# A channel-attention, causal-attention and two-layer network kernel: six images of a group as one schedule, and the first image's second normalisation moved into the attention

## The reference

```
x = x + proj(channel_attention(x))          # 8 heads; l2-normed q and k; 24 x 24 softmax per head
t = tokens(x)                               # 1024 x 192
t = t + causal_attention(layer_norm(t))     # 6 heads of 32, 1024 x 1024 scores, scale 1/sqrt(192)
z = layer_norm(t)
h = quant(z @ sign(W1).T + b1)              # 768 wide; 5 groups of W1's rows have their own mean
t = t + quant(gelu(h) @ sign(W2).T + b2)
x = image(t)
# quant: five groups of 6 images share one maximum (gamma): clip(a * 128 / (gamma + 1e-5), -128, 128);
#        images 30 and 31 belong to no group and get 0 from both quants
```

## Time and profile before

| | |
|---|---|
| Median of 3 runs | 4847.52 us (4846.21 to 4848.08) |
| Profiled execution | 4839.8 us, span 4838.0 us |
| Mean granted TensorE clock | 0.963 |
| Busy: PE, PE weight loads, DVE, ACT, POOL | 4119.7, 2991.4, 3333.5, 2714.9, 363.5 us |
| DMA | 161.62 MB, mean 33 GB/s |

### The profile page before, as it was taken

The page is one execution under the profiler, slowest core; times in us unless marked ns, Lnnn a source line. Parts: engine busy times, 40 slices in busy tenths (PEclk is TensorE's granted clock), DMA queues, the critical chain, the costliest instruction groups (busy, mean ns, idle before and its releaser), DMA issues.

```text
span 4838.0 us, 114787 instructions
## 1 busy us (share of the span) xinstructions
PE 4119.7 (85%) x39153; PEld 2991.4 (62%) x39208; DVE 3333.5 (69%) x6327; ACT 2714.9 (56%) x5911; POOL 363.5 (8%) x374
## 2 busy tenths in 40 slices
PE   3889887888898878989897979898888989887978
PEld 2666665566666636766674566666646666664565
DVE  3667676677676757767676777676667767676776
ACT  1555555555555555555556555565555555556655
POOL 0000002000000020000002000000020000002000
PEclk8999999999999989999999999999999999999999
DMA  1211111011111201111111011122101111111011
GB/s 49 52 35 34 35 34 34 0 47 35 35 34 40 55 0 40 34 35 34 35 36 32 0 47 34 35 49 46 34 0 40 34 35 34 35 41 27 0 40 41
DMA packets 48698, 161.62 MB, mean 33 GB/s; under 512 B 12420, under 2 KB 12934, under 8 KB 48006
## 3 DMA queue, kind: packets, MB, share of 16 engines
q1 hardware_dynamic: 48134, 154.39, 13.3%
HBM read 28.52 MB, written 25.17 MB: 11 GB/s over the span
## 4 chain that ended last, share of the span: by engine, by line
PE 61%; DVE 15%; issue 15%; ACT 4%; POOL 2%; DVEq 1%; DMA 1%; ACTq 0%; SPq 0%; POOLq 0%
PE PT L667 10%; PE OUT L687 9%; PE S L653 5%; PE PT L776 5%; PE S L703 4%; DVE nmax L1137 4%; DVE work L370 4%; PE S L613 3%; PE FR L613 3%; PE S L745 2%; PE FR L561 2%; PE S L561 2%; DVE XT L1032 1%; PE FR L620 1%; PE S L620 1%
## 5 line engine op out<-in xcount | busy, mean ns | idle before, releaser
L886 ACT ACTIVATE work<-S,nmax 128x256 f32<-128x256 f32 (+7 forms) x1536 | 1139.0, 742 | 1119.1 <-DVE nmax L1137 1056.7
L1137 DVE TENSOR_REDUCE nmax<-S 128x1 f32<-128x256 f32 (+7 forms) x1536 | 1156.4, 753 | 844.8 <-PE S L655 829.0
L667 PE MATMUL PT<-ident,work 128*128 128x128 f32 x6912 | 1110.2, 281 | 220.1 <-DVE work L370 188.7
L667 PEld LDWEIGHTS PT<-ident,work 128*128 128x128 f32 x6912 | 748.4, 142 | 434.6 <-DVE work L370 262.6
L370 DVE COPY work<-PT 128x512 f32<-128x512 f32 (+3 forms) x1536 | 892.0, 582 | 57.6 <-PE PT L667 52.7
L653 PE MATMUL S<-KS,QS 128*128 128x512 f16 (+3 forms) x1152 | 330.3, 342 | 106.8 <-issue 57.8
L890 ACT ACTIVATE work<-PT 128x512 f32<-128x512 f32 (+3 forms) x768 | 331.4, 432 | 53.5 <-PE PT L667 53.4
L655 PE MATMUL S<-causal,identb 128*128 128x128 bf16 x1536 | 341.7, 222 | 0.0
L653 PE MATMUL S<-odd 128*128 128x512 f16 (+3 forms) x1152 | 315.4, 328 | 16.7 <-ACT work L886 14.7
L1172 DVE TENSOR_REDUCE gm<-S 128x1024 f32 (+1 forms) x180 | 220.0, 1222 | 154.6 <-PE S L745 154.4
L745 PE MATMUL S<-odd,W1b 128*128 (+1 forms) x1080 | 297.4, 385 | 12.1 <-ACT odd L920 9.5
(11 more groups left out here) (198 smaller groups left out, 6037.7 us busy)
## 6 DMA issues: line engine op xcount, KB each, us to landing
X<-in_x SPq DMA_DIRECT2D x32, 768.0 KB, 5.3
odd<-hi_z SPq DMA_DIRECT2D x128, 192.0 KB, 4.2
odd<-odd SPq DMA_DIRECT2D x128, 192.0 KB, 4.2
out_y<-work SPq DMA_DIRECT2D x64, 384.0 KB, 3.9
QS<-hi_z SPq DMA_DIRECT2D x64, 192.0 KB, 3.6
QS<-odd SPq DMA_DIRECT2D x64, 192.0 KB, 4.0
KS<-hi_z SPq DMA_DIRECT2D x64, 192.0 KB, 4.7
KS<-odd SPq DMA_DIRECT2D x64, 192.0 KB, 4.7
```

The source lines that it names most:

```text
L667: last = tr(bank[:, P * (j - c0):P * (j - c0) + P], PS[m % 2][:, m // 2 % 2, P * j:P * j + P], ident[:, :])
L886: A(PS[n % 2][:, n // 2 % 2, 0:w], S[:, n % 2, 0:w], ACT.Exp, bias=nmax[:, n % MAXES:n % MAXES + 1], accum_out=rowsum[:, sum_col(n):sum_co ...
L1137: v.tensor_reduce(nmax[:, n % MAXES:n % MAXES + 1], S[:, n % 2, 0:P * (qtile(n) + 1)], AX.X, ALU.max, negate=True).then_inc(max_made, 1)
```

## The change

1. The slots are written out for all six images of a group (`GROUP` = 6, 288 units, 296 slots) and no inner loop runs over pairs; `groups` calls the body once a group. Images 30 and 31 keep the two-image form: `attention(LAST, 2, 1)`. All semaphore counts go by group and image (`after(g, u, per, n)`).
2. `EARLY` lays parts of the tail into the last slots of the six-image form. On DVE: the first image's statistics in slots 270 and 271 and their aggregate in 272, the second image's in 283, 284 and 285. On ACT: the first image's normalisation and rounding in 277 and 278. On PE and ACT: its four turns and copies in 286 to 289. Scores end with slot 287. The turns use the two banks of the front (`FB`) and the rounded parts a new place `zcat0` in `odd`, in KS1's first heads, which are read for the last time in slot 263. On POOL the first image's part is written out ahead of the loop over the other five.
3. In the tail, PE no longer waits for the last `add_to_t1`, but for the last exponential and oT copy, makes no turns before the loop over y1, and goes to y1 at once. ACT waits for the stacking DMAs and then normalises images 1 to 5. DVE makes no statistics ahead of the first maximum.

```diff
+EARLY = {270: "stats0", 271: "stats1", 272: "aggregate", 277: "norm0", 278: "norm1", 283: "next_stats0",
+         284: "next_stats1", 285: "next_aggregate", 286: "turn0", 287: "turn1", 288: "turn2", 289: "turn3"}
...
+zcat0 = odd[:, 6144:9216].rearrange("p (a b) -> p a b", a=TT)
...
             with e.Fori(0, NGROUPS) as g:
-                with e.Fori(0, GS // 2) as p:
-                    body(e.snap(g * (GS // 2) + p), p)
+                body(g)
                 tail(g)
...
 # POOL, tail
+                ln2(g * GS, zcat0)
+                with pool.Fori(1, GS) as b:
+                    ln2(pool.snap(g * GS + b), zcat)
...
 # PE, at the end of a slot
+                    if images == GS and EARLY.get(n, "").startswith("turn"):
+                        k = int(EARLY[n][-1])
+                        if k < 2:
+                            wait_freed(pe, g, GS, STEPS[k - 2])
+                            pe.wait_ge(z2lo_made, after(g, 0, 2, 3))
+                        else:
+                            pe.wait_ge(z2lo_made, after(g, 0, 2, 4))
+                            pe.wait_ge(z2t_made, after(g, 0, 4, k - 1))
+                        turn_z(FB[k % 2], k, zcat0).then_inc(z2t_full, 1)
...
 # PE, tail
-                pe.wait_ge(t1_step, nb * (GS // 2 * 3 * NB2))
+                pe.wait_ge(exp_made, nb * (GS * UNITS))
+                pe.wait_ge(oT_made, nb * (GS * NBI))
...
-                for k in range(4):
-                    turn_z2(g * GS, k)
...
 # ACT, at the end of a slot
+                    if images == GS and EARLY.get(n, "").startswith("norm"):
+                        act.wait_ge(rstd2_made, after(g, 0, 4, 4))
+                        norm_z2(0, g * GS, int(EARLY[n][-1]), zcat0)
+                    if images == GS and EARLY.get(n, "").startswith("turn"):
+                        k = int(EARLY[n][-1])
+                        put_z2(0, g * GS, k, FB[k % 2])
...
 # ACT, tail
-                with act.Fori(0, GS) as b:
+                for st in stacked:
+                    act.wait_ge(st, (g + 1) * (GS * STACKS) + STACKS)
+                    alone(act)
+                with act.Fori(1, GS) as b:
...
 # DVE, at the end of a slot
+                    if images == GS and n in EARLY:
+                        part = EARLY[n].removeprefix("next_")
+                        b = int(part != EARLY[n])
+                        if part == "stats0" and b:
+                            dve.wait_ge(ln2_step, after(g, 0, 16, 16))
+                            alone(dve)
+                        if part.startswith("stats"):
+                            stats2(b, range(4 * int(part[-1]), 4 * int(part[-1]) + 4))
+                        elif part == "aggregate":
+                            aggregate2(g * GS + b)
...
 # DVE, tail
-                for b in range(2):
-                    if b:
-                        dve.wait_ge(ln2_step, g * (GS * 16) + 16)
-                    stats2(b, range(TT))
-                    aggregate2(g * GS + b)
```

More of the change, by code:

```diff
@@ L74, in unit_of, with last_slot, triples_at, batches_at @@
     return 6 * (k // 2) + k % 2 + 2 * hh
[L77 to L84, removed]
+def last_slot(images):
+    return 12 * (NBI * images - 1) + BACK_AT
+def triples_at(images, slot):
+    return [k for k in range(KI * images) if 6 * (k // 2) + PV_AT[k % 2] == slot]
+def batches_at(images, slot, at):
+    return [j for j in range(NBI * images) if 12 * j + at == slot]
 def batch_tiles(j):
@@ L332, in groups, with after, wait_freed @@
             with e.Fori(0, NGROUPS) as g:
-                with e.Fori(0, GS // 2) as p:
-                    body(e.snap(g * (GS // 2) + p), p)
+                body(g)
                 tail(g)
[L337 to L343, removed]
+        LAST = NGROUPS
+        def after(g, u, per, n):
+            return g * (GS * per) + (u * per + n)
+        def wait_freed(e, g, u, step, less=0):
             b = bank_of(step)
-            e.wait_ge(front_free[b], after(pair, u, FRONT_FREES[b], freed(step) - less))
-        def of_pair(pair, per, n):
-            return pair * per + n
+            e.wait_ge(front_free[b], after(g, u, FRONT_FREES[b], freed(step) - less))
         def fronts_at(slot, run, parts, fronts):
@@ L420, in _, with body @@
             front(0, 0, True)
-            def pair_body(pair, p):
-                for u in range(2):
-                    front(pair, u + 1, True)
+            def body(g):
+                for u in range(GS):
+                    front(g, u + 1, True)
             def group_tail(g):
@@ L493, in _, with body, ln2 @@
             front(0, 0)
-            def pair_body(pair, p):
-                for u in range(2):
-                    front(pair, u + 1)
+            def body(g):
+                for u in range(GS):
+                    front(g, u + 1)
             def group_tail(g):
-                with pool.Fori(0, GS) as b:
-                    ab = pool.snap(g * GS + b)
+                def ln2(ab, zc):
                     pool.wait_ge(ln2_step, ab * 16 + 16)
@@ L521, in group_tail @@
                 pool.partition_all_reduce(gam2, run2, P, RMAX).then_inc(gam2_made, 1)
-            groups(pool, pair_body, group_tail)
+            groups(pool, body, group_tail)
             front(LAST, 1)
@@ L549, in front_part @@
                     if k == 0:
-                        pe.wait_ge(x_in, after(pair, u, 16, 16))
+                        pe.wait_ge(x_in, after(g, u, 16, 16))
                     for t in range(2):
@@ L585, in front_part @@
                 elif name == "u":
-                    pe.wait_ge(xsoft, after(pair, u, XSOFT, XSOFT))
+                    pe.wait_ge(xsoft, after(g, u, XSOFT, XSOFT))
                     for j in range(2):
@@ L605, in front_part @@
                     if k % 2 == 0:
[L606 removed]
+                        pe.wait_ge(zlo_made, after(g, u, 2, k // 2 + 1))
                     last = turn_z(FR, k)
@@ L825, in front_part @@
                 if name == "xexp":
-                    act.wait_ge(xsoft, after(pair, u, XSOFT, 6))
+                    act.wait_ge(xsoft, after(g, u, XSOFT, 6))
                     for j in range(2):
```

297 lines of the change are left out of this document (148 added, 149 removed).

## The result

| | before | after |
|---|---|---|
| Median | 4846.86 us (4846.07 to 4848.08, 4 runs) | 4679.76 us (4676.95 to 4687.25, 4 runs) |
| Profiled execution | 4839.8 us, span 4838.0 | 4680.1 us, span 4678.3 |
| Mean granted TensorE clock | 0.963 | 0.977 |

The ratio is 0.9657, interval 0.9641 to 0.9674: 167 us less in the medians and 159.7 us less in the two profiled executions.

The account below looks back on a forecast made before the run. PE, busy 85% of the span, was taken as the main bound, with DVE and ACT sharing the attention's chain. Seams 82 us plus tail 59 us gave 141, so 4699 us profiled and 4706 us median, range 4676 to 4758.

Parts of the forecast that it names:

- The seams: Ten seams between image pairs within groups become the step inside a pair: 8.23 us net each, 82 us in all.
- so 1.89 us of work that stood in the drain comes back: First 12 units after a seam: 28.69 us against 26.80, so 1.89 us of each seam's 10.12 us gross gain is lost.
- y1(0) may start at 793.3: Tail's start: PE's first y1 matmul comes 0.8 us after the attention's last transpose, 16.7 us earlier than before.
- PE waits 0.5: Tail, second image: after two y1 blocks PE waits 0.5 us for POOL's subtraction, which ends at 797.3.
- The early work: Second normalisation work moved from the tail into a group's last attention slots costs 5.8 us a group, bounds 0 and 15.8.
- the shared port: DVE and POOL lock one port pair: at worst DVE is held for both early subtractions, 16 us in all, forecast 4722.
- The second rule: At the pair loop's jump back, a taken branch outside the fetched window must fetch its target first; straight code is prefetched.
- Serial: Rival: early work's DVE, ACT and PE time adds up whole, 15.8 us a group; gain 91, time 4757; chance 0.14.
- only the jump: Rival: at the seams only the jump's 3.3 us goes, the drain is not overlapped; gain 92, time 4756; chance 0.07.
- Absorbed: Rival: double-buffered scores let engines run ahead, so early work in the attention costs nothing; gain 170, time 4677; chance 0.11.
- the slower rival: Attention of 30 images granted clock 0.92 instead of 0.985, 416 us more at 1.2 GHz: 4900 us; chance 0.03.
- part 2: First image's second normalisation moved from tail into attention: 17.6 less 5.8, net 11.8 us a group, 59 us in all.

Follow-up runs that it names:

- experiment 4: The kernel before with its pair loop written out as straight code, drain and refill of each pair kept: 4788.96 us, ratio 0.9895 to the kernel before.
- part 1 alone: The changed kernel with `EARLY` emptied: six images as one schedule, nothing moved out of the tail; 4741.54 us, ratio 0.9794 to the kernel before.
- experiment 5: The changed kernel with its early work at other slots, three versions: 4676.22, 4674.15 and 4664.58 us.
- the first try: The changed kernel with all early work moved to other slots, statistics from 275, turns in 288 to 291: 4676.22 us, ratio 0.9665 to the kernel before.

## Why the prediction was right, step by step

**The seams, 82 us predicted, 98.8 measured.** The gross step was right: 12.88 in the mean became 2.64, 102.3 us over ten, with 101.2 predicted. What failed is the sentence "so 1.89 us of work that stood in the drain comes back", its size and its company. The images' sum should have grown by 18.9 us; it grew by 3.5 (3120.8 to 3124.4). Three things lie in it:
- The refill costs 2.77 us a seam, 27.7 in all, not 1.89. I had compared 26.80 us at a clock of 0.95 with 28.69 at 1.00; experiment 4 has both at 1.00.
- Against it, a clean image lost 0.45 us (the fourth of a group 0.21), some 12 us over 30 images, nearly all in the slots of `add_to_t1`. The register in T1's address is shown to cost about half of that; the cause of the other half is open.
- The images of before spent 123 us at 1.2 GHz, those of the six-image schedule 75. These 48 us go with the remaining 12 us. That size is plausible, since in the first twelve units 2.4 us at 1.2 GHz went with 26.80 - 25.93 = 0.87, but I didn't separate them further.

So the refill that was booked too low works against the gain (8.8 us), and the clock that was booked in it works for it; what the forecast left out was above all the 12 us of the second point.

Experiment 4 splits the same 98.8 us in another way: 54.4 come from writing the loop out (28.6 for ten jumps, 25.8 in the images, which are the address and the clock), and 44.4 from laying the drain beside the next image. The last is net: the ten steps shrink by 73.8 us, from 10.02 to 2.64 each, and the images give back 29.4.

**"y1(0) may start at 793.3", 0.8 us after the last transpose:** it starts 0.82 after it. "PE waits 0.5" at the second image's first turn: no wait. The chain to the third image's aggregate is 28.52 - 10.16 = 18.4 us shorter, with 17.6 predicted. From maximum to maximum, with the longer drain taken off, I had 17.1 a group; measured 18.3. Of the 1.2 us between them, 0.5 is the wait that didn't come; the rest was not traced.

**The early work, 5.8 us a group predicted, 5.3 + 0.80 measured.** The sum is right, its terms less so:

| term | predicted | measured |
|---|---|---|
| first statistics, 270 to 272 | 1.3 | 1.84 |
| first normalisation, 277 and 278 | 1.5 | 1.91 |
| second statistics, 283 to 285 | 1.5 | 1.42 |
| turns 0 and 1 | 1.0 | 0.14 (turn 0's transposes alone) |
| drain | 0.5 | 0.80 (with turn 1) |

For the first statistics DVE's idle time left 1.7 us, and I had taken 1.3 because later slots would absorb a part; they did not. But the stretch of slots 270 to 275 had 12.67 - 9.32 = 3.35 us of idle DVE, more than the 2.8 us put into it, and at its end, in slot 275, the bn_stats cost it nothing. So an engine's idle time in a window does not say at which slot it can be used. The turns cost so little in the stretch because turn 1 and the copies, on which I had ACT wait before the next exponential, came behind the last maximum, where the drain took them. The forecast also read 2.5 us of idle DVE in slots 283 to 287; the row gives 9.32 - 7.04 = 2.3, and no term hangs on it. Slots 270 to 295 took 6.1 us more, within the 5 to 7 that were to show it.

**The rules weighed.** The first was the shared port. The new profile has the ten early subtractions in one group, and they take 1.592 us each, as in the earlier trace rows:

```profile
L515 POOL TENSOR_TENSOR odd<-XT,odd 128x768 f16<-128x768 f32 x10 | 15.9, 1592 | 73.2 <-ACT odd L892 73.2
```

The 16 us that the shared port would have cost at its worst did not show: the early work took 26.5 us of the last images at full clock, as predicted without it, and every DVE instruction beside those ten subtractions lasted as long as its like elsewhere, to 0.01 us. The one DVE instruction that is longer beside POOL belongs to the front and is the same in both kernels: its second cast of 128x768 from float32 to float16 (L1059 after, L1037 before) begins 1.3 us after a subtraction of POOL and takes 0.70 to 0.72 us; the first one, with POOL idle, takes 0.55 to 0.57. The early work adds no such pair. The second rule, on a taken branch outside the fetched window (the Trainium skill, Runtime: NRT & Kernel Launch, Instruction fetch mechanics), agrees with the run in kind: straight code saved 2.86 us a seam, and the two DMA queues of instructions moved 0.66 MB less (6.57 instead of 7.23 in the pages of experiment 4 and before). No view shows the fetch at the seam itself. The drain behind the jump was the larger part, 10.02 - 2.64 = 7.38 us.

**The rivals.** Serial (4757) and only the jump (4756) are out: the early work costs 6.1 of 15.8 us, and part 1 alone is worth 100.9 us, where the jump is 28.6. Absorbed (4677) gave nearly the right time by the wrong way, since the early work isn't absorbed. The forecast itself was 26 us too high. 17 of them are the seams, and 4 the tail and the early work together (63.2 us gained instead of 59); 3 were lost again outside the groups. The remaining 7 are chance: I counted from a median that was 7.7 us above the profiled execution, and after has its median at the profiled execution (4679.8 and 4680.1). The clock went against the slower rival: the whole run spent 147 us less at 1.2 GHz. 94 of those 147 come with part 2 (307.3 to 213.7): the pause at the tail's start, granted 0.61, is gone. The attention's own stretches didn't multiply; they became fewer.

## What to carry to other kernels

When a seam is removed, compare the parts around it at the same granted clock, or the clock's share is booked as work. Look for what else changes with the loop: an address that becomes a constant took a register instruction out of the chain here, on an engine that is busy only 69% of the time. Work that is moved beside a tight chain of three engines is best tried in small pieces, and its place is found by trying: 2.8 us of DVE cost 1.84 us in slots 270 to 272, and five slots later the 2.1 us of statistics among them cost nothing in their own stretch (the next one grew by 1.01 us with the normalisation in blocks, and by 0.27 with it in pieces). Before a longer stretch is called the price of an edit, its clock has to be looked at: one short stretch at 1.2 GHz was worth 1.7 us in experiment 5, the first try's edit 0.9.

## What was unexpected of the hardware

- **An address held in a register.** A DVE instruction whose address came from a register started 0.11 to 0.12 us later than with a constant: the gap between two starts was 0.37 and 0.36 us against 0.25, with a register instruction of 0.05 to 0.06 us between them.
- **Blocks and pieces.** The same aggregate and normalisation took 2.92 us from the chain with ACT's part as two blocks of 2.7 us (17.56 against 14.64). With it in pieces of at most 0.98 us, half in that stretch and half in the next, they took 0.27 and at most 0.84.
- **A late start tied to a place in the code.** The fourth image of every group in straight code lost 0.24 us in one step, and one step of every pair in the loop some 0.19, where DVE's own sequencer came late; with a register in T1's address the first of these was gone and another image had one of 0.26.
- **The clock answers to pauses.** After 7.28 us of waiting, PE ran six transposes in 0.82 us instead of 0.50, with 1.49 us for three y1 matmuls instead of 0.81.
- **A jump's price.** Ten seams in straight code were all 10.02 us long; with the jump they were 12.76 to 13.05.
